# Second layer of a two-layer transformer kernel: a turn cut into four stages, with norms and probabilities transposed in blocks and carried through DRAM

## What is computed

```python
h = layernorm(x) * (1 + ca) + sa
for i in range(4):                                  # DEPTH
    y = layer_norm(h, ln1_g[i], ln1_b[i])
    q, k, v = y @ Wq[i], y @ Wk[i], y @ Wv[i]       # 8 heads of 32
    lo = local_attn(q[:4], k[:4], v[:4])            # causal, own window of 128 and the one before
    go = causal_linear_attn(q[4:], k[4:], v[4:])    # buckets of 64, cumulated contexts
    h = h + concat(lo, go) @ Wo[i] + bo[i]
    y = layer_norm(h, ln2_g[i], ln2_b[i])
    h = h + gelu(y @ W1[i] + b1[i]) @ W2[i] + b2[i] # 256 -> 1024 -> 256
x = x + ga * h
```

## Time and profile before

| | us |
|---|---|
| median of 3 runs | 3123.42 (3123.28 to 3123.43) |
| the profiled execution | 3120.52 |
| its span in the trace | 3118.7 |
| TensorE busy in the span | 2921.5 (94%) |
| VectorE, ScalarE, GpSimd busy | 1676.6, 1415.3, 827.9 |
| this layer on TensorE, from the first projection to the last down product | 717.85 to 2465.84 |

### The profile page before, as it was taken

How to read it: one execution, slowest core, us unless ns; L and a number is a source line. 1 busy time by engine, 2 the same in 40 slices (tenths; PEclk the granted TensorE clock), 3 DMA queues, 4 the chain that set the end, 5 groups by cost and what they waited for, 6 DMA issues and landing times. The chain is left out here.

```text
span 3118.7 us, 53260 instructions
## 1 busy us (share of the span) xinstructions
PE 2921.5 (94%) x20742; PEld 1958.5 (63%) x20742; DVE 1676.6 (54%) x5013; ACT 1415.3 (45%) x3117; POOL 827.9 (27%) x829
## 2 busy tenths in 40 slices
PE   6889999888999999999999999999999788799998
PEld 3566666664666666565666666665656444468887
DVE  4677776755655545545445444456555478641112
ACT  3666666633445354444444453544444134132224
POOL 1001111113323322322323223233333310025552
PEclk8999999999999999999999999999999899899999
DMA  4111111002000112010211000110100000023325
GB/s 140 18 19 19 18 19 19 13 3 72 25 28 18 38 31 69 28 55 28 67 47 35 21 14 28 32 55 20 38 20 25 11 1 28 27 68 80 75 84 189
DMA packets 102249, 126.48 MB, mean 41 GB/s; under 512 B 12451, under 2 KB 79014, under 8 KB 100960
## 3 DMA queue, kind: packets, MB, share of 16 engines
q1 hardware_dynamic: 93168, 102.56, 11.4%
q0 software_dynamic: 7680, 16.32, 2.1%
q10 hardware_dynamic: 1152, 4.19, 0.3%
HBM read 75.56 MB, written 43.61 MB: 38 GB/s over the span
## 5 line engine op out<-in xcount | busy, mean ns | idle before, releaser
L1435 PE MATMUL bank<-h2T,w 128*128 128x512 f32 x1024 | 478.8, 606 | 5.2 <-ACT gT L1373 3.7
L1473 PE MATMUL bank<-w,gT 128*128 128x256 f32 x2048 | 465.9, 381 | 0.0
L1473 PEld LDWEIGHTS bank<-w,gT 128*128 128x128 f32 x2048 | 379.3, 190 | 49.7 <-issue 0.5
L1090 POOL TENSOR_TENSOR prob<-prob,rsum 128x512 f32<-128x512 f32 (+1 forms) x256 | 237.9, 950 | 592.4 <-DVE rsum L1245 592.4
L1435 PEld LDWEIGHTS bank<-h2T,w 128*128 128x128 f32 x1024 | 182.2, 190 | 223.8 <-issue 173.6
L1373 ACT ACTIVATE gT<-bank,vec 128x512 f32<-128x512 f32 x256 | 175.1, 687 | 285.5 <-PE bank L1435 284.0
L609 ACT ACTIVATE y<-y,least 128x128 f32<-128x128 f32 (+3 forms) x512 | 252.0, 554 | 50.6 <-DVE least L479 50.6
L479 DVE CUSTOM_DVE_ANT_0 y<-bank,mask 128x128 f32<-128x128 f32 (+3 forms) x512 | 223.9, 485 | 70.2 <-PE bank L706 68.9
L1222 DVE CUSTOM_DVE_ANT_0 prob<-bank,mask 128x256 f32<-128x256 f32 (+1 forms) x512 | 164.3, 387 | 168.3 <-PE bank L1425 168.3
L1336 ACT ACTIVATE prob<-prob,least 128x256 f32<-128x256 f32 (+1 forms) x512 | 239.6, 471 | 15.8 <-DVE least L1222 15.5
L1251 DVE COPY probT<-bank 128x1024 f32<-128x1024 f32 (+1 forms) x128 | 138.4, 1082 | 189.7 <-PE bank L1489 189.7
(11 more groups left out here) (328 smaller groups left out, 5050.2 us busy)
## 6 DMA issues: line engine op xcount, KB each, us to landing
turned_rows<-score SPq DMA_DIRECT2D x124, 128.0 KB, 2.3
score<-turned_rows SPq DMA_DIRECT2D x31, 512.0 KB, 3.6
w<-in_W SPq DMA_DIRECT2D x8, 1024.0 KB, 7.6
expert_parts<-zeros SPq DMA_DIRECT2D x8, 1024.0 KB, 6.1
we<-in_we SPq DMA_DIRECT2D x16, 512.0 KB, 5.0
rows<-modulation SPq DMA_DIRECT2D x40, 128.0 KB, 3.5
x<-in_x SPq DMA_DIRECT2D x8, 512.0 KB, 6.3
prob<-score SPq DMA_DIRECT2D x64, 64.0 KB, 2.3
```

The costliest lines, as they stand in the source:

```text
L1090: nc.gpsimd.tensor_tensor(two, two, rsum[:, at:at + 2].unsqueeze(2).to_broadcast([P, 2, width]), ALU.mult).then_inc(s["probs"], 1)
L1435: ins = nc.tensor.matmul(M[m % 2][:, :], w1[:, k, m * P:(m + 1) * P], h2T[:, k, :], start=(k == 0), stop=(k == KD - 1))
L1473: ins = nc.tensor.matmul(M[i][:, (t % 2) * D:(t % 2 + 1) * D], gT[:, m, t * P:(t + 1) * P], w2[:, m, :], start=(m == 0), stop=(m == MF - 1))
```

## The change

Turns stay, but each now holds four stages of different sequences: scores and linear attention of turn g; values and out projection of turn g - 1; the hidden product and gelus of turn g - 2; the down product of turn g - 3. The loops run over 35 turns (`TURNS + STAGES`) instead of 33.

- TensorE loses both kinds of transposes: `turn` for the second norm (it stays for the very first turn) and all of `probs_turn`. The second norm now takes the way of the first: `turn_rows` on VectorE, DMAs through DRAM (`move_rows`), gain on ScalarE out of the same tile that the first norm's columns use.
- The probabilities take a way of that kind too: `turn_probs` transposes 32x32 blocks on VectorE into two new tiles, and `move_probs` writes each to DRAM in four DMAs (768 KB for windows 0 and 1, 1 MB for windows 2 and 3) and reads it back in one. `probs_out` goes. `values` reads its moving operand from the arriving tile in four runs of 32 columns where it had 128 in a row.
- v of the local heads gets its own double-buffered tile (`vloc`), linear attention's output a double-buffered one; the out projection goes to banks S[2], S[3] instead of V.
- TensorE's order: project, down 0 to 3, scores, down 4 to 11, scores, down 12 to 16, linear turn and context, down 17 to 26, linear out, values, down 27 to 31, out projection, then the eight hidden products without a break.
- VectorE, ScalarE, GpSimd and SP are reordered to match; weight loads move to later turns; the clearing of the experts' rows is 32 DMAs of 256 KB, two a turn.
- While the later stages are still empty, 4 idle products stand in each of two places in turns 0 to 2.

The core of the diff (in the loops and in the functions that moved, only the lines that stand afterwards are shown):

```diff
+        vloc = sb("v_local", [P, 2, NT, P])
...
+        pblocks = [sb(f"prob_blocks{h}", [P, GROUPS, n, SQUARE]) for h, n in enumerate(PROBS)]
...
+        def block_of(q, m, j):
+
+            return q // 2, j if q == 0 else (0, 4, 0, 8)[q] + 2 * j + m
...
+            def move_rows(away, done, arrived):
                 for i in range(GROUPS):
+                    src = rblocks[SQUARE * i:SQUARE * (i + 1), :, :, :].rearrange("p a t r -> p a (t r)")
+                    sp.dma_start(by_group[i], src).then_inc(away.sem, 16)
+                away.wait(sp, done)
+                sp.dma_start(xT, by_feature).then_inc(arrived.sem, 16)
+
+            def move_rows1(i):
+                sp.wait_ge(s["rows_turned"], rows1_turned(i))
+                if i >= 3:
+                    turned2_in.wait(sp, 16 * (i - 2))
+                elif i == 2:
+                    turned1_in.wait(sp, 16)
+                if i >= 3:
+                    sp.wait_ge(s["h2_gain"], 2 * (i - 2))
+                elif i == 2:
+                    sp.wait_ge(s["h1_gain"], 4)
+                move_rows(turned1_away, 16 * GROUPS * i, turned1_in)
+
+            def move_rows2(h):
+                sp.wait_ge(s["rows_turned"], rows2_turned(h))
+                if h + 2 < TURNS:
+                    turned1_in.wait(sp, 16 * (h + 2))
+                    sp.wait_ge(s["h1_gain"], 2 * (h + 3))
+                else:
+                    turned2_in.wait(sp, 16 * h)
+                    sp.wait_ge(s["h2_gain"], 2 * h)
+                move_rows(turned2_away, 16 * GROUPS * (h + 1), turned2_in)
+
+            def move_probs(g, h):
+                sp.wait_ge(s["probs_turned"], 4 * g + 2 * h + 2)
+                if g:
+                    probs_in[h].wait(sp, 16 * g)
+                    sp.wait_ge(s["av_full"], g)
+                dram = c.probs_dram[h]
+                for i in range(GROUPS):
+                    src = pblocks[h][SQUARE * i:SQUARE * (i + 1), :, :, :].rearrange("p a k r -> p a (k r)")
+                    sp.dma_start(dram[:, :, i, :].rearrange("a p n -> p a n"), src).then_inc(probs_away[h].sem, 16)
+                probs_away[h].wait(sp, 16 * GROUPS * (g + 1))
+                sp.dma_start(probT[h].rearrange("p i k r -> p (i k r)"), dram.rearrange("a p i n -> (a p) (i n)"))\
+                  .then_inc(probs_in[h].sem, 16)
...
                 if g + 1 < TURNS:
-                    move_turned1(g + 1)
-                if e and b == 0:
-                    sp.wait_ge(s["hidden_full"], MF * B * e)
-                    load_w1(e)
+                    move_rows1(g + 1)
+                if g < TURNS:
+                    move_probs(g, 0)
+                    move_probs(g, 1)
...
+                if 1 <= g <= TURNS:
+                    move_rows2(g - 1)
...
+                if g + 1 < TURNS:
+                    bias_o(g + 1)
+                if 1 <= g <= TURNS:
+                    rstd("stats2", g, "rstd2")
+                    bias_2(g - 1)
...
+            def turn_probs(g, q):
+                n = len(keys_of(q))
+                first = block_of(q, 0, 0)[1]
+                dve.wait_ge(s["probs"], 8 * g + 2 * q + 2)
+                if g and q % 2 == 0:
+                    probs_away[q // 2].wait(dve, 16 * GROUPS * g)
+                src = prob[:, 4 * q:4 * q + 4, from_col(q):PAIR]
+                if n == 2:
+                    src = src.rearrange("p j (m a f) -> p (j m) a f", m=n, f=SQUARE)
+                else:
+                    src = src.rearrange("p j (a f) -> p j a f", f=SQUARE)
+                nc.vector.transpose(out=pblocks[q // 2][:, :, first:first + 4 * n, :].rearrange("p a k r -> p k a r"),
+                                    in_=src).then_inc(s["probs_turned"], 1)
...
-                    nc.vector.tensor_tensor(ys, ys, V[i][:, :].rearrange("p (t n) -> p t n", t=2), ALU.add)\
+                    nc.vector.tensor_tensor(ys, ys, S[:, 2 + i, :].rearrange("p (t n) -> p t n", t=2), ALU.add)\
...
+            for g in range(TURNS + STAGES):
+                last = g - 1 - STAGES - (TURNS - B)
+                if g < TURNS:
+                    linear_in(g)
+                if g + 1 < B:
+                    stats_x(g + 1)
+                if last >= 0:
+                    stats_x(B + last)
+                if g < TURNS:
+                    masked(g, (0, 1))
+                    linear_mid(g)
+                    invert(g, 0)
+                    masked(g, (2, 3))
+                    invert(g, 1)
+                if g + 1 < B:
+                    modulate(g + 1)
+                if last >= 0:
+                    modulate(B + last)
+                if g < TURNS:
+                    context_sum(g)
+                if g + 1 < TURNS:
+                    nxt = c.y[:, (g + 1) % B]
+                    if g + 1 < B:
+                        dve.wait_ge(s["modulated"], g + 2)
+                    else:
+                        dve.wait_ge(s["w2_added"], 2 * (g + 2 - B))
+                    stats(nxt, "stats1")
+                if g < TURNS:
+                    turn_probs(g, 0)
+                    invert(g, 2)
+                if g + 1 < TURNS:
+                    if g:
+                        dve.wait_ge(s["rows_turned"], rows1_turned(g + 1) - 1)
+                    else:
+                        dve.wait_ge(s["turn1_full"], 2)
+                    norm(nxt, "rstd1", g + 2, "norm1")
+                    if g >= 2:
+                        turned2_away.wait(dve, 16 * GROUPS * (g - 1))
+                    elif g == 1:
+                        turned1_away.wait(dve, 16 * GROUPS)
+                    turn_rows("norm1", g + 2)
+                if g < TURNS:
+                    turn_probs(g, 1)
+                if g >= STAGES:
+                    mlp_sum(g - STAGES, 0)
+                if g < TURNS:
+                    invert(g, 3)
+                    turn_probs(g, 2)
+                if g >= STAGES:
+                    mlp_sum(g - STAGES, 1)
+                if g < TURNS:
+                    turn_probs(g, 3)
+                if 1 <= g <= TURNS:
                     before = c.y[:, (g - 1) % B]
                     attn_sum(g - 1)
                     dve.wait_ge(s["op_added"], 2 * g)
                     stats(before, "stats2")
+                    dve.wait_ge(s["rows_turned"], rows2_turned(g - 1) - 1)
                     norm(before, "rstd2", g, "norm2")
                     if g + 1 < TURNS:
+                        turned1_away.wait(dve, 16 * GROUPS * (g + 1))
+                    else:
+                        turned2_away.wait(dve, 16 * GROUPS * (g - 1))
+                    turn_rows("norm2", g)
...
+                if g >= 2:
+                    turned2_in.wait(act, 16 * (g - 1))
+                    gains_in(g - 2, h2T, 2 * KD, "h2_gain")
+                if g < TURNS:
                     exps(g, 0)
+                    exps(g, 1)
                     act.wait_ge(s["qlT_full"], g + 1)
                     nc.scalar.copy(qlT[:, :], V[0][:, :]).then_inc(s["qlT_out"], 1)
+                    exps(g, 2)
+                    exps(g, 3)
+                    linear_away(g)
+                if 1 <= g <= TURNS:
+                    values_away(g - 1)
+                for m in range(MF):
+                    if m == MF // 2 and g + 1 < TURNS:
+                        turned1_in.wait(act, 16 * (g + 1))
+                        gains_in(g + 1, hT[:, :, 1:1 + T], 0, "h1_gain")
+                    if g >= 2:
+                        h = g - 2
+                        act.wait_ge(s["hidden_full"], MF * h + m + 1)
+                        nc.scalar.activation(gT[:, m, :], M[m % 2][:, :], ACT.Gelu,
+                                             bias=vec[:, h // B, 4 * KD + m:4 * KD + m + 1])\
+                          .then_inc(s["gelu_done"], 1)
...
+                    if t >= 2 and g >= 2:
+                        pe.wait_ge(s["op_added"], 2 * (g - 2) + t - 1)
...
-                        pe.wait_ge(s["op_added"], 2 * (g - 1) + i + 1)
+                        linear_out_away.wait(pe, g)
...
+                elif g:
+                    pe.wait_ge(s["w2_added"], 2 * (g - 1) + m + 1)
...
             def values(g):
                 for q in range(4):
+                    if q % 2 == 0:
+                        probs_in[q // 2].wait(pe, 16 * (g + 1))
                     keys = keys_of(q)
                     for m, key in enumerate(keys):
                         for j in range(4):
+                            part, k = block_of(q, m, j)
                             ins = nc.tensor.matmul(S[32 * j:32 * j + 32, 0, q * P:(q + 1) * P],
+                                                   vloc[:, g % 2, key, 32 * j:32 * j + 32],
+                                                   probT[part][:, :, k, :],
                                                    start=(m == 0), stop=(m == len(keys) - 1),
                                                    tile_position=(0, 32 * j))
                 ins.then_inc(s["av_full"], 1)
 
```

(55 more changed lines are left out.)

308 lines of the change are left out of this document (95 added, 213 removed).

## The result

The changed kernel takes 3025.86 us (median of 4 runs, 3022.14 to 3030.53) against 3123.35 (4 runs, 3120.08 to 3123.43): ratio 0.9691 [0.9674, 0.9709], 97.5 us or 3.1% less. The forecast was 3012, its range 2985 to 3065.

A forecast was written before the change was run, and what follows sets the result against it. TensorE, busy 1578.2 of 1590 us, was taken as the bound. Fill 140, turns 3 to 31 1418.7 and drain 78 gave a layer of 1636.7 against 1748.0, 111.3 less: 3012 us, range 2985 to 3065.

The forecast's parts named there:

- TensorE's 48.7 us a turn: TensorE in a steady turn: period falls from 53.5 to 48.7 us, ends 47.3 and 49.5.
- The transposes' 4.1: TensorE, steady turn: removing the second norm's transposes (0.97 us) and the probabilities' (3.15) saves 4.1 us.
- the two waits' 0.85: TensorE, steady turn: waits for the attention output's copy and the transposed probabilities go, 0.85 us a turn.
- the gelu wait: TensorE waiting for gelus, 1.3 us a turn: at least part should go, but no gain was booked.
- rival 3: TensorE's values: reading in four runs of 32 columns stops parallel heads, 4.1 us a turn, 3143 us; 4 in 100.
- Block transposes at 1.25: VectorE: each block transpose of 1024 columns takes 1.25 us, or 2.5 at the upper end beside GpSimd's multiplies.
- Modulating turns, 0.8 each: VectorE's order in eight of turns 3 to 31 has no slack left: 0.8 us each, ends 0 and 3.
- Fill, 140: Turns 0 to 2 of the layer: 42, 45 and 50 us plus 3 for slow pieces, 140 us.
- Drain, 78: After turn 31: remaining down, hidden, values and out projection, 75.1 us, plus 3 for uncovered gelus, 78 us.
- Weight loads, booked at nothing: Weight loads move to turns whose tile's last reader is done and next reader 5 us or more away; no cost.
- DRAM, 7 us of slack: First norm's trip through DRAM: columns arrive near 39, TensorE needs them applied at 48.7, some 7 us slack, no cost.
- Rival 2: DRAM trip ends last and the kernel is slower, once the trip takes 19 us; 3150 us at 20 to 21; 4 in 100.

The follow-up runs named there:

- experiment 1: Kernel before the change, order unchanged, with 30 of a turn's 36 TensorE transposes left out (stale values): 3039.24 us, ratio 0.9717.
- experiment 2: Changed kernel with 36 identity transposes added on TensorE ahead of each turn's first hidden product: 3142.05 us, ratio 1.0046.
- Experiment 7: Changed kernel with GpSimd multiplying window 1's probabilities before it takes the root for the next norm: 3025.44 us, ratio 0.9674.
- Experiment 6: Changed kernel with the modulation of a sequence moved to the end of a turn: 3006.7 us, ratio 0.9612.
- experiment 9: Changed kernel with modulation at turn's end, window 1 multiplied before the root, idle products at seams, second norm's rows and w2 moved earlier on SP: 2994.41 us, ratio 0.9565.
- experiment 4: Changed kernel with normed rows' trips one round of writes longer and the second norm's rows ahead of the second probabilities trip: 3138.76 us, ratio 1.003.
- experiment 5: Changed kernel with longer row trips, second norm's rows between probabilities' trips, first norm's gain before gelu 6, w2 loaded right after first norm's rows: 3024.2 us, ratio 0.969.

## Why the prediction was right

By its own steps:

- **TensorE's 48.7 us a turn.** 48.5 measured. The transposes' 4.1 and the two waits' 0.85 left the turn; experiments 1 and 2 move 2.7 and 3.9 us with 30 and 36 transposes, in either direction. That the gelu wait gives nothing back was booked rightly, though the wait itself shrank, from 1.3 us a turn to 5.1 us in 20 turns: the hidden products take 13.83 us where their pieces took 14.61, but the down products' pieces take 14.51 where they took 13.92. The Trainium skill, "VectorE: DVE Perf Modes", Rules for kernel authors, advises TensorE for a transpose of 128x128 whose result may go to PSUM. Following it costs this kernel, whose TensorE has no time to spare, 3.9 us a turn (experiment 2).
- **Values in pieces, cost nothing** (rival 3): 1.67 us from start to start where it was 1.96 with a wait of 0.35 (2.03 in the earlier trace rows is the duration).
- **Block transposes at 1.25** (end 2.5): 1.219 and 1.246 us on the mean. GpSimd's instructions beside them don't lengthen them: 1.20 at 1590.36 with GpSimd idle, 1.21 and 1.25 at 1592.14 and 1594.38 beside it. The rule of the Trainium skill that only instructions with both port pairs or two SBUF inputs are locked out ("SBUF — State Buffer", Who interferes with whom) agrees with that; it names `tensor_scalar`, the norm's operation, among those that can take both pairs. GpSimd does slow the norm, to 4.19 us where the prediction kept 2.8; in a steady turn the other waits in VectorE's order just took it. Experiment 7 shows where the norm's length comes from, and that its 1.4 us are worth at most 0.1 a steady turn (48.4 for 48.5).
- **Modulating turns, 0.8 each.** The right place and the wrong size: 1.4 to 2.3 a turn, in two of eight 4.0 and 4.6. TensorE in turns 3 and 4:

```profile
902.14 15.67 PE L1521 MATMUL bank<-h2T,w 128*128 128x512 f32 x32 [2.02 <-issue]
...
954.26 6.30 PE L1521 MATMUL bank<-h2T,w 128*128 128x512 f32 x14 [1.75 <-issue]
```

  The pause is 2.02 and 1.75. In turns 3 and 5 (pauses of 2.02 and 2.01) the 32 hidden products then take 15.67 instead of 14.02, the granted clock 0.89 from 902 to 918; in turn 4 it is 1.00. All eight take 408.3 us, 20.0 above eight steady turns of 48.53, where 6.4 was booked. Experiment 6 shows the cause: with the modulation elsewhere they are 48.5.
- **Fill, 140.** 145.0: 45.1, 46.5 and 53.5 where 42, 45, 50 and 3 for slow pieces were booked. The seams cost about what was booked (3.0 and 1.9 for the clock, 3 each booked), and the first projection of turn 0 itself took 8.67 instead of 7.11. Turn 2 is 3.5 above its 50 by the wait of 6.44 us for the context. For turn 2 the prediction named neither of its two causes, the trip of the second norm and the modulation; experiment 6 takes away the second and turn 2 is 50.0, experiment 9, among other things, both, and it is 44.3.
- **Drain, 78.** 77.5 (2375.03 - 2297.49).
- **Weight loads, booked at nothing.** Turns 11, 19 and 27 cost 1.1, 0.6 and 3.9 us. TensorE in turn 27, whose granted clock is 0.83 from 2056 to 2066, behind the pause:

```profile
2055.93 2.53 PE L1558 MATMUL bank<-w,gT 128*128 128x256 f32 x8 [2.03 <-DMA w<-in_W]
```

  SP issues the second weights behind both probability trips. Experiments 4 and 5 show both sides: some 15 us a time when the trips are longer, 0.1 to 0.2 when the load is issued first.
- **DRAM, 7 us of slack.** This step was wrong, though its result, no cost, was right. It measured the slack to TensorE's use; the real deadlines are places in the lists of ScalarE and SP. Its own layout had ScalarE at the first norm's gain at 43 and the columns there at 39; measured, they are 42.5 and 40.8. In the steady turn shown ScalarE's gain of the second norm is already late:

```profile
1571.55 1.52 ACT L1421 ACTIVATE h2T<-score,vec 128x512 f32<-128x512 f32 x2 [0.42 <-DMA score<-turned_rows]
```

  So it is in 18 of the 20 steady turns, 25.9 us in all. TensorE does not feel it (the wait of 2.57 us at 1428.05 stands in a turn of 48.5). So ScalarE's own slack is used up there, and what is left lies behind it, between the exponentials and the context. At the first norm the slack is about 1.6 us: the load issued at 1594.17 lands some 4.2 later, at 1598.4, and ScalarE comes to it at 1551.49 + 48.5 = 1600.0. Rival 2 was therefore closer than its condition says: not at a trip of 19 us but with one more round of writes (3.7 us alone, 5.0 beside the probabilities, 1566.27 to 1571.28 in that kernel) the kernel is slower than before.

The sum: 1655.6 against 1636.7, 18.9 too much: 20.0 - 6.4 = 13.6 from modulating turns, 5.0 from the fill, 5.5 from weights, less 29 x 0.17 = 4.9 of the steady period and 0.5 of the drain; the rest is rounding. The profiled execution is 19.5 us above the forecast for it, the median only 13.9 above its own: it stands 2.9 below its profiled execution, where 2.9 above was carried over from before. That part of the nearness is luck.

## What to carry to other kernels

Where one engine is at 99%, count what sits on it and could be done by one at half load, and price a turn by that: the five microseconds were right to 0.2. Then measure the slack of each moved transfer to the place in the list of the engine that waits for it, on every queue that it passes, and not to the use of the data; and walk the turns that do something extra one by one. Moving a wait on an in-order list is cheap: here it bought some 25 us for the modulation, and let a longer trip cost nothing in a steady turn.

## What the runs showed of the hardware that was not expected

- A pause of 2 us of TensorE cost up to 1.65 us more behind it by a lower granted clock, but not each time: 2.02 and 2.01 did (turns 3 and 5), 2.09 (at 2132.80, products 14.02) and 1.75 did not. What tells them apart stays open.
- The same four writes of 128 KB and their completion took 3.7 us, or 7.3 when a load of probabilities had just been issued (1559.61).
- GpSimd's multiplies slowed VectorE's norm: its four instructions took 1.38 us beside none, 2.75 to 2.82 beside two and 4.19 beside four. Block transposes stayed at 1.20 to 1.25 with them or without. The modulation's first four instructions (two tensors in) took 3.21 us beside a multiply and 1.65 without.
